# Scatters of routed rows sent two or three per slot, with waits between them, in an attention and mixture-of-experts kernel

## The reference

```python
x = x + _L0_xattn_ref(_layernorm(x), ctx_1024, mask, mask, Wq, Wkv, Wc)      # 32 batches x 128 tokens x 128, 16 heads of 8
x = x + _L0_ffn_ref(_layernorm(x), router_w, w1, b1, w2, b2)
# in _L0_ffn_ref, xf = the 4096 tokens:
logits = jnp.einsum('td,ed->te', xf, router_w)                               # 8 experts
top_vals, top_idx = jax.lax.top_k(logits, 2)
probs = jax.nn.softmax(top_vals, axis=-1)
for e in range(8):
    w = jnp.sum(jnp.where(top_idx == e, probs, 0.0), axis=-1)
    h = jax.nn.gelu(jnp.einsum('td,fd->tf', xf, w1[e]) + b1[e], approximate=False)
    y = jnp.einsum('tf,df->td', h, w2[e]) + b2[e]
    out = out + w[:, None] * y
```

## Time and profile before

| | us |
|---|---|
| median of 3 runs | 504.89 |
| lowest, highest | 502.22, 506.77 |
| the profiled execution, and its span from first to last instruction | 509.84, 507.7 |
| busy: PE, weight loads, DVE, ACT, POOL | 368.2, 285.6, 281.1, 230.5, 224.6 |
| the 64 scatters of routed rows (L632), busy | 63.0 |
| the 71 scatters of results (L681), busy | 70.8 |

### The profile page before, as it was taken

One profiled execution on the slowest core, in us unless ns is written; L12 is line 12 of the kernel. 1 busy time (PEld: TensorE's weight loads), 2 busy tenths in 40 slices (PEclk: granted clock), 3 DMA queues, 4 the chain that ended last, 5 costly groups with the idle time before them and its releaser, 6 DMA issues.

```text
span 507.7 us, 12389 instructions
## 1 busy us (share of the span) xinstructions
PE 368.2 (73%) x3715; PEld 285.6 (56%) x3715; DVE 281.1 (55%) x883; ACT 230.5 (45%) x536; POOL 224.6 (44%) x316
## 2 busy tenths in 40 slices
PE   2548889797979878585596400899898999998900
PEld 1133556464646545363364300899797998887900
DVE  7167998779666766554343762344343444443426
ACT  1314677667364654433354100466454665554500
POOL 7883422312370724334607471255453555444520
PEclk9999998879786798775767555899998999999965
DMA  4795345635242332010101023555565655565358
GB/s 125 176 254 156 98 119 108 151 85 139 79 123 77 103 96 71 26 40 29 43 5 38 23 68 96 162 168 182 158 181 161 180 174 171 159 184 167 95 163 334
DMA packets 57119, 63.00 MB, mean 124 GB/s; under 512 B 14109, under 2 KB 40116, under 8 KB 56896
## 3 DMA queue, kind: packets, MB, share of 16 engines
q1 hardware_dynamic: 51584, 53.22, 37.9%
q0 software_dynamic: 4320, 8.47, 4.9%
q10 hardware_dynamic: 1152, 0.53, 0.4%
HBM read 37.65 MB, written 11.88 MB: 98 GB/s over the span
## 4 chain that ended last, share of the span: by engine, by line
PE 40%; DVE 14%; SPq 13%; issue 9%; DMA 9%; another core or an unknown queue 7%; ACT 5%; ACTq 0%; POOLq 0%; POOL 0%; DVEq 0%
PE smax L1117 9%; PE sexp L1126 8%; DVE shift L1186 5%; PE tail L950 5%; PE smax L906 5%; DMA stacks<-dispatch_d 4%; PE feed L985 3%; SPq L409 2%; SPq L493 2%; SPq L486 2%; SPq L494 2%; PE feed L897 2%; ACT probs L752 2%; SPq L487 2%
## 5 line engine op out<-in xcount | busy, mean ns | idle before, releaser
L1186 DVE TENSOR_REDUCE shift<-smax 128x4 f32<-128x512 f32 x128 | 85.9, 683 | 68.3 <-PE smax L906 41.2
L752 ACT ACTIVATE probs<-sexp 128x512 f32<-128x512 f32 x128 | 73.9, 593 | 41.6 <-PE sexp L914 29.5
L632 POOL DMA_INDIRECT dispatch_d<-rows_out,row_i x64 | 63.0, 984 | 64.1 <-DVE row_i L1338 47.5
L681 POOL DMA_INDIRECT result_d<-y_out,stacks x71 | 70.8, 997 | 38.4 <-issue 36.4
L1557 DVE TENSOR_TENSOR probs<-smax,b_cols 128x512 f32<-128x512 f32 x71 | 49.1, 691 | 68.3 <-PE smax L1117 66.4
L1117 PE MATMUL smax<-probs,w_ring 128*128 128x128 f32 x568 | 81.7, 289 | 3.8 <-ACT probs L857 1.7
L1126 PE MATMUL sexp<-w_sb,probs 128*128 x568 | 79.0, 283 | 1.0 <-ACT probs L861 1.0
L1117 PEld LDWEIGHTS smax<-probs,w_ring 128*128 128x128 f32 x568 | 71.7, 198 | 11.6 <-issue 10.3
L906 PE MATMUL smax<-stacks 64*128 64x128 bf16 x512 | 59.5, 250 | 23.6 <-DVE shift L1186 10.5
L1126 PEld LDWEIGHTS sexp<-w_sb,probs 128*128 128x128 f32 x568 | 70.5, 195 | 2.6 <-issue 1.4
L906 PEld LDWEIGHTS smax<-stacks 64*128 64x128 bf16 x512 | 34.6, 107 | 54.4 <-issue 22.2
(11 more groups left out here) (191 smaller groups left out, 528.6 us busy)
## 6 DMA issues: line engine op xcount, KB each, us to landing
w_ring<-w_t_dram SPq DMA_DIRECT2D x71, 256.0 KB
stacks<-kpart SPq DMA_DIRECT2D x48, 128.0 KB
stacks<-qpart SPq DMA_DIRECT2D x48, 128.0 KB
stacks<-dispatch_d SPq DMA_DIRECT2D x71, 65.0 KB
stacks<-result_d SPq DMA_DIRECT2D x16, 256.0 KB, 5.4
ctx<-ctx_t_dram SPq DMA_DIRECT2D x8, 256.0 KB, 3.2
w_sb<-w_t_dram SPq DMA_DIRECT2D x8, 256.0 KB
out_dram<-xs SPq DMA_DIRECT2D x8, 256.0 KB, 5.9
```

The lines of the kernel that those rows point to most:

```text
L632: nc.gpsimd.indirect_dma_start(out=dispatch_d, out_offset=bass.IndirectOffsetOnAxis(ap=row_i[r % RR][:, k, b:b + 1], axis=0), in_=rows_out ...
L681: nc.gpsimd.indirect_dma_start(out=result_d, out_offset=bass.IndirectOffsetOnAxis(ap=xg[r][:, D + 1:D + 2].bitcast(U32), axis=0), in_=y_ou ...
L752: nc.scalar.activation(dst, sexp[hp][:], ACT.Exp).then_inc(exp_done, 1)
L1186: nc.vector.tensor_reduce(shift4[n % 2][:, hp, 0, 4 * m:4 * m + 4], smax[hp][:], AX.X, ALU.max, negate=True).then_inc(max_taken, 1)
```

## The change

The two bursts of each of the rounds 0 to 5 become a table: for each slot, which round sends how many scatters. The first scatter of a slot goes at once; before the n-th (n = 2, 3, 4) POOL waits for the slot's n-th `take_max`, and in slots 32 to 34, which have none, for the n-th `exp` of the slot's batch. In slots 35 and 36 there is neither, and the function waits for nothing. Round 5's eight scatters now stand in slots 35 and 36, behind `copy_rows(6)` of slot 35. Rounds 6 to 8 are sent as before.

```diff
-SEND_AT = (17, 21, 25, 28, 30, 34)
-SEND2_AT = (19, 23, 27, 29, 31, 35)
+SEND_COUNT = {18: ((0, 2),), 19: ((0, 2),), 20: ((0, 2),), 21: ((0, 2),),
+              22: ((1, 2),), 23: ((1, 2),), 24: ((1, 2),), 25: ((1, 2),),
+              26: ((2, 3),), 27: ((2, 3),), 28: ((2, 2),), 29: ((3, 3),), 30: ((3, 3),), 31: ((3, 2), (4, 1)),
+              32: ((4, 3),), 33: ((4, 3),), 34: ((4, 1),), 35: ((5, 4),), 36: ((5, 4),)}
...
-            def send_rows(r, ks):
+            def send_ready(r):
 
                 routed(pool, r, ROUTE_STEPS)
                 pool.wait_ge(rows_placed, TOPK * (r + 1))
                 pool.wait_ge(rows_normed, ROUNDS[r + 1])
                 pool.wait_ge(rows_copied, r + 1)
...
+            def send_row(r, n):
+
+                k, b = divmod(n, many(r))
+                nc.gpsimd.indirect_dma_start(
...
+            def pace(s, u):
+
+                if s < BATCH:
+                    pool.wait_ge(max_taken, UNITS * s + u)
+                elif s - LAG < BATCH:
+                    pool.wait_ge(exp_done, UNITS * (s - LAG) + u)
+
+            sent = [0] * ROUND
...
-                if s in SEND_AT:
-                    send_rows(SEND_AT.index(s), (0,))
-                if s in SEND2_AT:
-                    send_rows(SEND2_AT.index(s), (1,))
+                n = 0
+                for r, count in SEND_COUNT.get(s, ()):
+                    if sent[r] == 0:
+                        send_ready(r)
+                    for _ in range(count):
+                        n += 1
+                        if n > 1:
+                            pace(s, n)
+                        send_row(r, sent[r])
+                        sent[r] += 1
```

More of the change, by code:

```diff
@@ L629, in send_rows @@
                 pool.wait_ge(rows_copied, r + 1)
[L630 to L634, removed]
+            def send_row(r, n):
+                k, b = divmod(n, many(r))
+                nc.gpsimd.indirect_dma_start(
+                    out=dispatch_d, out_offset=bass.IndirectOffsetOnAxis(ap=row_i[r % RR][:, k, b:b + 1], axis=0),
+                    in_=rows_out[r % RR][:, b, k, :], in_offset=None).then_inc(rows_sent[r % RR], 16)
+            def pace(s, u):
[4 more added lines that the diff above has]
+            sent = [0] * ROUND
             for s in range(LAST_SLOT + 1):
@@ L661, in _, with send_all @@
                     copy_rows(r)
-                if s in SEND_AT:
-                    send_rows(SEND_AT.index(s), (0,))
-                if s in SEND2_AT:
-                    send_rows(SEND2_AT.index(s), (1,))
+                n = 0
[8 more added lines that the diff above has]
+                        sent[r] += 1
+            def send_all(r):
+                send_ready(r)
+                for n in range(TOPK * many(r)):
+                    send_row(r, n)
             row_scale(7)
@@ L669, in _ @@
             row_scale(8)
-            send_rows(6, (0, 1))
+            send_all(6)
             place_rows(8)
-            send_rows(7, (0, 1))
-            send_rows(8, (0, 1))
+            send_all(7)
+            send_all(8)
             def store_tile(t, r, first=False):
```

## The result

The changed kernel took 484.10 us (median of 4 runs, 483.63 to 486.34), the kernel before beside it 505.83 us (4 runs, 502.22 to 506.90). The ratio is 0.959, with a 95% interval of 0.953 to 0.965: the medians differ by 21.7 us. The profiled execution of the kernel before (509.84 us) was longer than all four of these; 4.2 us of its distance to the changed kernel's (484.44 us, span 482.4) lie ahead of slot 13, where nothing was changed.

The account below looks back on a forecast made before the run. Scatter bursts were taken to stall PE, ACT and DVE. Recovered 22, less 3, 3.5 and 1, gave 14.5, say 15 us: 495 on the profiled 509.84, 490 on the median of 504.89; range 478 to 504.

Parts of the forecast that it names:

- The mechanism: In the attention slots, POOL's scatters in a row stall PE, ACT and DVE; up to 28.3 us in the loop.
- My chance of 0.18 for no change: Rival: cost goes with scatter count, or groups of three and short slots stall like bursts; 499 to 506 us, chance 0.18.
- The excess of 28.3 us: Slots 17 to 31: time beyond the scatter-free slots 13 to 16 (26.49 us), the most that bursts could cost.
- PE's lower clock: PE's matmuls in the loop: 8.2 us of the excess might have other causes; without it 20.1 us remained.
- Pairs in slots 18 to 25 at nothing: Slots 18 to 25: 16 scatters leaving in pairs cost other engines nothing; if wrong, 11 us.
- Groups of three in slots 26 to 31, 3 us (0 to 9): Slots 26 to 31: the third scatter of a close group may stall PE; 3 us lost, range 0 to 9.
- The expert stage: Evidence that spaced scatters cost others nothing: 64 scatters in 152 us, with PE busy 143.6 us.
- Slots 32 to 34, 3.5 us lost: Short slots 32 to 34 get seven scatters instead of one; 3.5 us lost, range 0 to 5.
- The new waits of POOL at nothing: POOL's waits for maxima delay its later work harmlessly: nothing, or up to 1 us at each of two places.
- ACT's longest wait without a releaser: Sign of being right: ACT's longest wait with unknown releaser falls from 8.6 to about 2 us.
- The end, +1 us (-1 to +5.2): Slots 35 and 36: round 5's eight scatters behind round 6's copy shift the end by +1 us, range -1 to +5.2.
- the slower rival: Eight unbroken scatters in slots 35 and 36 halt round 6's routing, 5.2 us on the chain; 510 us, chance 0.10.

Follow-up runs that it names:

- the run of eight: Eight more scatters in a row in slot 14, shown on the kernel before with waits also put into its own bursts: 501.57 us, ratio 0.992.
- the heavy condition: Sessions in which the unchanged kernel before took about 505 us (medians 504.96 and 504.38 in the experiments).
- the light condition: Sessions in which the unchanged kernel before took about 464 to 466 us (medians 463.83 to 466.84).
- changed_again: The changed kernel, unaltered, measured once more beside the kernel before: 465.97 us against 466.84, ratio 1.000.
- the stretches without halts: Median of five halt-free traces, of kernels with a run of eight or waits added: 26.3 us for slots 17 to 21, 22.2 for 28 to 32.
- the three traces with additions: Changed kernel plus eight spaced scatters in slots 13 to 16, or eight plain transfers or multiplications in slot 14: 479.90, 477.61, 483.11 us.
- run_then_waits_b: Second run of the kernel before with eight more scatters in a row in slot 14 and waits for maxima within its own bursts: 501.57 us, ratio 0.992.

## Why the prediction was right, step by step

The forecast was 490 us with 478 to 504; it came to 484.10. Taken from slot 13 on, its sum was 14.5 us against 21.1 measured.

**The mechanism** (bursts halt PE, ACT and DVE) is shown, by the run of eight in the heavy condition. That the forecast came true was in part luck: I read one execution and took the halts for a property of the kernel. Had the measurement fallen on the light condition, the answer would have been "no change" (ratio 1.000, changed_again), and no row of the trace of before would have warned of it. My chance of 0.18 for no change had other reasons.

**The excess of 28.3 us** for slots 17 to 31 was a fair price. Against the stretches without halts, the kernel before lost 34.3 us from 17 to 32 (5.5, 3.4, 7.9 and 17.5). My reference, slots 13 to 16, was right for the four-slot stretches and too long for slots 29 to 31. I took 22 of it back as recoverable, less 3 for groups of three: 19. Measured: 22.9. *This is the term that was too small, by 4 us.* I had cut it because of PE's lower clock; that clock came back with the halts gone (0.84 from 99.58 to 230.92 in the changed kernel, 0.78 in the same stretch of before):

```profile
99.58:230.92 131.34, 104.90 (x1445) 73.20 (x1438) 99.12 (x354) 75.30 (x182) 55.15 (x69) 0.84 0.31 85
```

**Pairs in slots 18 to 25 at nothing:** 1.6 and 0.6 us over the stretches without halts, about as much as those differ among themselves (25.1 to 27.4 and 25.2 to 27.6). Right in size; the reason given, that a pair is short of the third scatter at which a halt begins, is not borne out, since in the run of eight ACT's first wait began with the first scatter. **Groups of three in slots 26 to 31, 3 us (0 to 9):** 3.6 and 5.5 over, 9.1, at the upper end (4.8 to 8.2 in the three traces with additions); they run together across slots, as the rows above show. The expert stage was the right evidence for spaced scatters and the wrong one for these.

**Slots 32 to 34, 3.5 us lost:** from round 5's product to the end of ACT's `norm_rows(6)` it took 16.6 us (230.92 to 247.51) after 12.7 (258.65 to 271.39), 3.9 lost. Right in place and size.

**The new waits of POOL at nothing:** no wait at `place_rows` in the whole trace, and no engine that waits for POOL from 125 to 256 us. Right. Of the signs that I had named, one failed: ACT's longest wait without a releaser was to fall to about 2 us and was 4.26.

**The end, +1 us (-1 to +5.2):** from the same `norm_rows(6)` to round 7's product it took 15.7 us after 17.0, so -1.3, just outside. The halt that the slower rival priced didn't come: in the run of eight ACT had one wait of 1.31 us with no releaser. PE has little to do there; the product of round 6 was copied 3.2 us after the rows, where it took 8.5. Then 4.0 us of that were given back, for the reason named in the prediction: `row_scale(7)` stands behind the eight scatters, at 258.23, and the chain waits for it. The first send of round 6 came 14.0 us after the rows; the prediction had 14.3 for the case without a halt.

```profile
257.25 0.96 POOL L636 DMA_INDIRECT dispatch_d<-rows_out,row_i  x1 [0.30 <-issue]
258.23 0.89 POOL L607 TENSOR_TENSOR rstd<-var_eps,minus_half 128x3 f32<-128x3 f32 x1
...
261.51 1.06 POOL L636 DMA_INDIRECT dispatch_d<-rows_out,row_i  x1 [1.06 <-DVE row_i L1361]
```

**The sum by what was measured:** 22.9 - 3.9 + 1.3 = 20.3, and 0.7 in the stretch without scatters and 0.1 behind round 7: 21.1.

**The Trainium skill** states ("DMA: Bandwidth & Descriptors", Anatomy of one DMA) that one can emit a lot of descriptors before the incremental cost shows up. It says so of the time of one DMA; that the other engines pay nothing either was my reading of it. The reading fits the light condition, where ACT's longest wait that ended in a run of eight was 0.28 us, and not the heavy one, where ACT waited 7.45 us.

**Still open:** what sets the heavy condition, by which path scatters then slow the other engines, and how much of the gain is the table's and how much the waits'. No edit of the kernel made the one or the other condition.

## What to carry to other kernels

A stall whose releaser no record shows, on several engines at once, has a cause of its own: find the instruction that runs during all of them. Spacing by a wait on another engine's progress works only if the scatters' own inputs are there before that progress is made; put it a slot after its inputs, or the waits are fulfilled on arrival and the burst is back, as in the first burst of run_then_waits_b. And measure on more than one occasion: this change is worth 4% or nothing, and one profile cannot say which.

## What the runs showed of the hardware that I had not expected

The same program on the same chip takes 464 us in one session and 504 in another (chip 10), with all executions of a session within some 3%; the halts lie where POOL makes indirect transfers in a row, and SP is slowed beside them too (9.2 to 10.7 us against 4.4 to 4.5 for four issues by SP beside them). Eight plain transfers of 128 rows of 520 bytes are issued by POOL in 4.54 us, eight indirect ones in 10.05.
